# First delta product ahead of x's transposes, and the experts' start positions summed on VectorE

## The reference

```
out  = einsum(x, W_base) + b_base                       # btc,oc->bto
h    = einsum(x, As)                                    # btc,erc->bter
x    = x + out + einsum(h, Bs, w) * 2.0                 # bter,eor,be->bto

w, sel = top_k(softmax(cond), 2);  w = w / w.sum()      # per sequence
dense_w = zeros(B, 8).at[rows, sel].add(w)
mlp(x, g, u, d) = (gelu_tanh(x @ g) * (x @ u)) @ d      # 128 -> 512 -> 128
x = x + mlp(x, shared) + sum_e dense_w[:, e] * mlp(x, expert e)
```

## Time and profile before

| what | us |
|---|---|
| device time, three runs | 130.02, 130.43, 130.75 (median 130.43) |
| device time of the profiled execution | 130.85 |
| its span | 129.2 |
| TensorE busy | 124.9 (97% of the span), 873 products |
| VectorE busy | 90.2 (70%) |
| ScalarE busy | 72.0 (56%) |
| GpSimd busy | 61.8 (48%) |

### The profile page before, as it was taken

The page is one execution under the profiler, slowest core; times in us unless marked ns, Lnnn a source line. Parts: engine busy times, 40 slices in busy tenths (PEclk is TensorE's granted clock), DMA queues, the critical chain, the costliest instruction groups (busy, mean ns, idle before and its releaser), DMA issues.

```text
span 129.2 us, 3167 instructions
## 1 busy us (share of the span) xinstructions
PE 124.9 (97%) x873; PEld 113.9 (88%) x873; DVE 90.2 (70%) x177; ACT 72.0 (56%) x136; POOL 61.8 (48%) x111
## 2 busy tenths in 40 slices
PE   6999999999999999999999999999999999999991
PEld 5948887878887888998999999999999999999990
DVE  1686798769979999633377768667867686766731
ACT  2349677976956877113466485648565846711110
POOL 5364974463797877453344632643364604610000
PEclk9999999999999999999999999999999999999999
DMA  2998778799100077679745686558699960014922
GB/s 39 266 329 313 218 272 219 296 310 292 36 3 0 5 173 239 233 275 411 302 183 223 244 322 231 208 223 325 228 315 306 402 211 0 3 26 141 263 82 61
DMA packets 14524, 26.56 MB, mean 206 GB/s; under 512 B 2224, under 2 KB 7600, under 8 KB 12976
## 3 DMA queue, kind: packets, MB, share of 16 engines
q1 hardware_dynamic: 14048, 26.28, 60.8%
q10 hardware_dynamic: 464, 0.13, 0.4%
HBM read 12.52 MB, written 1.31 MB: 107 GB/s over the span
## 4 chain that ended last, share of the span: by engine, by line
PE 97%; issue 0%; DVE 0%; DVEq 0%
PE bank L1059 11%; PE bank L1100 9%; PE bank L1101 9%; PE bank L1099 9%; PE bank L1081 6%; PE bank L1004 6%; PE bank L1005 6%; PE bank L1006 6%; PE bank L1121 5%; PE bank L1122 4%; PE bank L1123 4%; PE bank L1022 3%; PE bank L928 3%; PE bank L936 3%; PE bank L1023 3%; PE bank L1024 3%
## 5 line engine op out<-in xcount | busy, mean ns | idle before, releaser
L558 ACT ACTIVATE work<-bank 128x512 f32<-128x512 f32 x48 | 28.7, 599 | 38.3 <-PE bank L1101 17.6
L720 DVE TENSOR_TENSOR bank<-bank,work 128x512 f32<-128x512 f32 x40 | 27.9, 698 | 18.3 <-PE bank L1101 13.1
L739 DVE TENSOR_TENSOR hT_lo<-bank,hT_hi 128x512 fp32r<-128x512 f32 x40 | 27.3, 682 | 1.0 <-issue 0.5
L1099 PE MATMUL bank<-xp,wst 128*128 128x256 f32 x96 | 27.2, 284 | 0.0
L1101 PE MATMUL bank<-xp,wst 128*128 128x256 f32 x96 | 27.2, 283 | 0.0
L1100 PE MATMUL bank<-xp,wst 128*128 128x256 f32 x96 | 27.2, 283 | 0.0
L485 POOL TENSOR_TENSOR wstd<-wexd,wstd 128x512 fp32r<-128x512 f32 x12 | 15.6, 1296 | 24.0 <-ACT wstd L600 24.0
L567 ACT CAST hT_hi<-bank 128x512 fp32r<-128x512 f32 x40 | 23.3, 583 | 1.8 <-DVE bank L720 1.8
L1099 PEld LDWEIGHTS bank<-xp,wst 128*128 128x128 f32 x96 | 18.4, 192 | 0.0
L1100 PEld LDWEIGHTS bank<-xp,wst 128*128 128x128 f32 x96 | 18.4, 192 | 0.0
L1101 PEld LDWEIGHTS bank<-xp,wst 128*128 128x128 f32 x96 | 18.4, 192 | 0.0
(11 more groups left out here) (156 smaller groups left out, 214.0 us busy)
## 6 DMA issues: line engine op xcount, KB each, us to landing
wst<-wex SPq DMA_DIRECT2D x12, 1024.0 KB, 5.0
raw_ex<-n_L_cond_skill_gate_dram SPq DMA_DIRECT2D x8, 256.0 KB, 3.5
raw_ex<-in_L_cond_skill_up_dram SPq DMA_DIRECT2D x8, 256.0 KB, 4.1
sst<-n_L_cond_skill_gate_dram SPq DMA_DIRECT2D x8, 256.0 KB, 3.5
sst<-in_L_cond_skill_up_dram SPq DMA_DIRECT2D x8, 256.0 KB, 4.0
xn<-in_x_dram SPq DMA_DIRECT2D x4, 256.0 KB, 4.8
out_dram<-xT SPq DMA_DIRECT2D x4, 256.0 KB, 2.7
sst<-_L_cond_shared_gate_dram SPq DMA_DIRECT2D x1, 256.0 KB, 4.9
```

Source lines behind the costliest of these rows:

```text
L558: act.activation(gelu_sb[q], gate_ps[q][:, :], ACT.Gelu_apprx_tanh).then_inc(gelu_done, 1)
L720: dve.tensor_tensor(up_ps[u][:, :], up_ps[u][:, :], gelu_sb[q], ALU.mult).then_inc(h_done, 1)
L739: dve.tensor_tensor(hT_lo[:, q, :], up_ps[u][:, :], f32(hT_hi[:, q, :]), ALU.subtract).then_inc(lo_done, 1)
L1099: pe.matmul(of_c, w_hi, x_hi, start=True, stop=False)
```

## The change

It makes two edits. In the first stretch of TensorE's program `delta_w(0)` stands ahead of x's first transposes and `delta_w(1)` ahead of `sort_counts`, and the warm-ups are (3, 1, 2). With it VectorE makes `w_eff(1)` right after `w_eff(0)` and the router's small operations after both, and ScalarE copies the counts after `copy_xT(0)` and a table load. The second edit computes the start positions with two small VectorE steps over `below`, a table of constants, and the products in `sort_starts`, `half`, `par` and ScalarE's copy of the result are gone. The second count product has its operands exchanged, so each partition holds all experts' sizes. The scratch of the new steps lies in `rows`, which is written later.

The diff, without most of its changes of semaphore counts and of declarations:

```diff
@@ -33,7 +33,7 @@
     NC = I // P
-    WARM_UP = (4, 2, 1)
+    WARM_UP = (3, 1, 2)
     DN = NC * H
...
@@ -92,6 +90,10 @@
         rows = sb("rows", [B, 2, 3, 32])
+        spare = rows[:, :, :, :].rearrange("b k v n -> b (k v n)")
+        n_ge = spare[:, 0:64].rearrange("b (e r) -> b e r", e=8)
+        in_front = spare[:, 0:144].rearrange("b (i f e) -> b i f e", i=2, f=9)
         wlist = sb("wlist", [P, 32])
...
@@ -333,23 +334,21 @@
             pool.memset(ones[:, :], 1.0).then_inc(const_fill, 1)
-            pool.memset(upick[:, :, :], 2.0).then_inc(const_fill, 1)
+            pool.memset(below[:, 0, :, :], 2.0).then_inc(const_fill, 1)
+            pool.memset(below[:, 1, :, :], 1.0).then_inc(const_fill, 1)
             pool.memset(ltri[:, :], 1.0).then_inc(const_fill, 1)
             pool.wait_ge(const_fill, 1)
             pool.affine_select(out=ident[:, :], in_=ident[:, :], compare_op=ALU.not_equal, fill=1.0,
                                base=0, pattern=[[-1, P]], channel_multiplier=1).then_inc(consts, 1)
             pool.iota(iota[:, :], pattern=[[1, 32]], base=0, channel_multiplier=0,
                       allow_small_or_imprecise_dtypes=True).then_inc(consts, 1)
-            pool.wait_ge(const_fill, 4)
+            pool.wait_ge(const_fill, 5)
             pool.affine_select(out=ltri[:, :], in_=ltri[:, :], compare_op=ALU.is_gt, fill=0.0,
                                base=0, pattern=[[1, B]], channel_multiplier=-1).then_inc(consts, 1)
-            pool.affine_select(out=upick[:, 0, :], in_=upick[:, 0, :], compare_op=ALU.is_gt, fill=0.0,
-                               base=0, pattern=[[1, 8]], channel_multiplier=-1).then_inc(consts, 1)
-            pool.affine_select(out=upick[:, 1, :], in_=upick[:, 1, :], compare_op=ALU.is_gt, fill=0.0,
-                               base=0, pattern=[[-1, 8]], channel_multiplier=1).then_inc(consts, 1)
-            pool.affine_select(out=upick[:, 2, :], in_=upick[:, 2, :], compare_op=ALU.is_equal, fill=0.0,
-                               base=0, pattern=[[-1, 8]], channel_multiplier=1).then_inc(consts, 1)
+            for i in range(2):
+                pool.affine_select(out=below[:, i, :, :], in_=below[:, i, :, :], compare_op=ALU.is_gt, fill=0.0,
+                                   base=0, pattern=[[1, 9], [-1, 8]], channel_multiplier=0).then_inc(consts, 1)
             pool.iota(thr[:, :], pattern=[[2, 8]], base=2, channel_multiplier=0,
...
@@ -396,22 +395,18 @@
             pool.memset(base[:, :, :], 0.0).then_inc(base_zero, 1)
-            pool.wait_ge(sort_sum, 2)
-            pool.tensor_scalar(par[:, :], half[:, :], -2.0, None, ALU.mult).then_inc(sort_step, 1)
-            pool.wait_ge(sort_step, 4)
-            pool.tensor_tensor(par[:, :], par[:, :], rank_n[:, 1, :], ALU.add).then_inc(sort_step, 1)
-            pool.wait_ge(sort_sb, 2)
-            pool.tensor_tensor(pos_e[:, 0, :], rank_n[:, 0, 0:8], starts[:, 2, :], ALU.subtract).then_inc(sort_step, 1)
-            pool.tensor_tensor(pos_e[:, 1, :], rank_n[:, 0, 0:8], starts[:, 0, :], ALU.add).then_inc(sort_step, 1)
+            pool.wait_ge(sort_sum, 5)
+            pool.tensor_tensor(pos_e[:, 1, :], rank_n[:, 0, 0:8], starts[:, 0, 0:8], ALU.add).then_inc(sort_step, 1)
+            pool.tensor_scalar(pos_e[:, 2, :], starts[:, 1, 0:8], starts[:, 0, 8:9], None, ALU.add).then_inc(sort_step, 1)
+            pool.wait_ge(sort_step, 5)
+            pool.tensor_tensor(pos_e[:, 2, :], pos_e[:, 2, :], pos_e[:, 1, :], ALU.subtract).then_inc(sort_step, 1)
             pool.wait_ge(sort_step, 6)
-            pool.tensor_scalar(pos_e[:, 0, :], pos_e[:, 0, :], 0.0, None, ALU.is_equal).then_inc(sort_step, 1)
+            pool.wait_ge(sort_sum, 6)
+            pool.tensor_tensor(pos_e[:, 2, :], pos_e[:, 0, :], pos_e[:, 2, :], ALU.mult).then_inc(sort_step, 1)
+            pool.wait_ge(sort_step, 7)
+            pool.tensor_tensor(pos_e[:, 3, :], pos_e[:, 1, :], pos_e[:, 2, :], ALU.add).then_inc(sort_step, 1)
             pool.wait_ge(sort_step, 8)
-            pool.tensor_tensor(pos_e[:, 2, :], pos_e[:, 0, :], starts[:, 1, :], ALU.mult).then_inc(sort_step, 1)
-            pool.wait_ge(sort_step, 9)
-            pool.tensor_tensor(pos_e[:, 3, :], pos_e[:, 1, :], pos_e[:, 2, :], ALU.add).then_inc(sort_step, 1)
-            pool.wait_ge(sort_step, 10)
             pool.tensor_tensor(pos_ke[:, :, :], memb[:, :, 0:8],
...
@@ -531,11 +526,11 @@
                                bias=bias[:, 0:1]).then_inc(x1hi_ready, 1)
-            act.wait_ge(sort_mm, 1)
-            act.copy(rank_n[:, :, :], count_ps[0:B, 0:2 * B].rearrange("p (a b) -> p a b", a=2)).then_inc(sort_sb, 1)
             copy_xT(0)
             act.wait_ge(exp_done, 1)
             act.activation(rt[:, 24:25], rt[:, 8:9], ACT.Gelu_apprx_tanh).then_inc(gelu_table, 1)
+            act.wait_ge(sort_mm, 1)
+            act.copy(rank_n[:, :, :], count_ps[0:B, 0:2 * B].rearrange("p (a b) -> p a b", a=2)).then_inc(sort_sb, 1)
             copy_xT(1)
...
@@ -579,19 +574,15 @@
                     gelu(t, c % 2)
-                    if g == 0 and c == 2:
-                        act.wait_ge(sort_mm, 2)
-                        act.copy(starts[:, :, :], start_ps[0:B, 0:24].rearrange("p (a b) -> p a b", a=3)
-                                 ).then_inc(sort_sb, 1)
                     if c > 1 or (c == 0 and g > 0):
                         split_h_hi(t - 1, (t - 1) % 2, (t - 1) % 3)
                     if g == 0 and c >= 2:
                         split_hi(0, c - 2)
                     if g == 1 and c == 2:
-                        act.wait_ge(sort_mm, 3)
+                        act.wait_ge(sort_mm, 2)
                         act.copy(left_rank[:, :], rank_ps[0:B, 0:4]).then_inc(sort_sb, 1)
                     if g == 3 and c == 0:
-                        act.wait_ge(sort_mm, 4)
+                        act.wait_ge(sort_mm, 3)
                         act.copy(wlist[:, :], list_ps[:, 64:96]).then_inc(lists_ready, 1)
...
@@ -694,15 +685,15 @@
             scale_B(1)
-            router_weights()
             dve.wait_ge(setup_ps, 3)
             dve.wait_ge(consts, 1)
             dve.tensor_tensor(wT[:, :], bank[6][:, 0:H], ident[:, :], ALU.add).then_inc(setup_sb, 1)
             dve.wait_ge(setup_sb, 3)
             w_eff(0)
+            w_eff(1)
+            router_weights()
             router_sum()
-            w_eff(1)
             w_eff(2)
...
@@ -769,14 +760,26 @@
                     if g == 0 and c == 0:
-                        dve.wait_ge(consts, 8)
+                        dve.wait_ge(consts, 7)
                         dve.wait_ge(sort_sb, 1)
-                        dve.tensor_tensor(n_ge[:, :, :],
-                                          rank_n[:, 1, :].rearrange("p (b a) -> p b a", a=1).to_broadcast([B, B, 8]),
-                                          thr[:, :].rearrange("p (a r) -> p a r", a=1).to_broadcast([B, B, 8]),
+                        n = rank_n[:, 1, 0:8]
+                        dve.tensor_tensor(n_ge, n.rearrange("p (e a) -> p e a", a=1).to_broadcast([B, 8, 8]),
+                                          thr[:, :].rearrange("p (a r) -> p a r", a=1).to_broadcast([B, 8, 8]),
                                           ALU.is_ge).then_inc(sort_sum, 1)
                         dve.wait_ge(sort_sum, 1)
-                        dve.tensor_reduce(half[:, :], n_ge[:, :, :], AXIS_X, ALU.add).then_inc(sort_sum, 1)
+                        dve.tensor_reduce(twos_odd[:, 0, :], n_ge, AXIS_X, ALU.add).then_inc(sort_sum, 1)
+                        dve.wait_ge(sort_sum, 2)
+                        dve.scalar_tensor_tensor(twos_odd[:, 1, :], twos_odd[:, 0, :], -2.0, n, ALU.mult, ALU.add
+                                                 ).then_inc(sort_sum, 1)
+                    if g == 0 and c == 1:
+                        dve.wait_ge(sort_sum, 3)
+                        dve.tensor_tensor(in_front, twos_odd[:, :, :].rearrange("p i (a e) -> p i a e", a=1)
+                                          .to_broadcast([B, 2, 9, 8]), below[:, :, :, :], ALU.mult).then_inc(sort_sum, 1)
+                        dve.wait_ge(sort_sum, 4)
+                        dve.tensor_reduce(starts[:, :, :], in_front, AXIS_X, ALU.add).then_inc(sort_sum, 1)
+                        dve.scalar_tensor_tensor(pos_e[:, 0, :], twos_odd[:, 0, :], 2.0, rank_n[:, 0, 0:8],
+                                                 ALU.mult, ALU.is_equal).then_inc(sort_sum, 1)
                     if g == 0 and c == 2:
...
@@ -939,21 +942,14 @@
             def sort_counts():
-                pe.wait_ge(consts, 8)
+                pe.wait_ge(consts, 7)
                 pe.wait_ge(sort_step, S_MEMB)
                 pe.matmul(count_ps[0:B, 0:B], ltri[:, :], memb_sum[:, :], start=True, stop=True)
-                pe.matmul(count_ps[0:B, B:2 * B], memb_sum[:, :], ones[:, 0:B], start=True, stop=True).then_inc(sort_mm, 1)
-            def sort_starts():
-                pe.wait_ge(sort_sum, 2)
```

(20 more changed lines are left out.)

39 lines of the change are left out of this document (18 added, 21 removed).

## The result

| | median, us | range, us | runs |
|---|---|---|---|
| kernel before | 130.38 | 130.02 to 130.75 | 4 |
| changed kernel | 131.50 | 131.12 to 131.71 | 4 |

The ratio is 1.0082, interval 1.0065 to 1.0098. The forecast was 130.3, "the same", with 131.0 as the top of the range. The changed kernel's profiled execution took 131.12 (span 129.4), 0.27 more than the one of before. The two traces can explain this 0.27; the other 0.8 of the medians' 1.1 is in neither trace, and needed experiments.

What follows compares the result with a forecast made beforehand. TensorE's row of work was taken to bound the kernel, with 97% of the chain. Terms -0.39 + 0.15 + 0.15 = -0.09 on 130.85, on the median 130.34, gave 130.3; range 129.5 to 131.0.

Steps and rivals of the forecast that it cites:

- the same: Whole kernel: the forecast verdict, no change that measurement can tell (about 0.5%, 0.65 us); chance 0.62.
- What bounds the kernel: Whole kernel: TensorE holds 97% of the chain of waits; other engines' idle time matters only if it delays TensorE.
- Step 1: First ten microseconds: delta(0) waits for sB(0) with its weight load exposed, 0.3 us of slow time lost, costing +0.15.
- rival A: Start of the kernel: the clock rises sooner or unseen gaps close, giving 129.6; chance 0.24.
- rival B: TensorE before 5.5 us: emptier early work makes the clock rise later; a rise at 10 gives 131.4; chance 0.11.
- Step 2: Around 20 us: the small start-position products leave TensorE and the first down product gets cheaper, -0.39.
- Step 3: Around 20 us: VectorE's added small operations delay lo(1), so TensorE waits some 0.2 at the second down product; +0.15.
- Rival C: Around 20 us: VectorE is the limit, lo(1) and lo(2) both 0.4 late, giving 130.6 to 130.8; chance 0.07.
- So it happens once: After the second down product: the next lo has some 0.2 to spare, so VectorE's lateness does not recur.
- GpSimd's part priced at nothing: GpSimd's queue: two operations fewer ahead of pos_ke, which comes no later, and constants ready long before needed; no cost.

Runs made afterwards that it cites:

- e5: Changed kernel with one wait added, so GpSimd starts x's fourth group only after VectorE's first pack; median 130.37 us, ratio to before 0.9932.
- e12: Changed kernel timed again as it is, twelve executions; median 131.18 us.
- e10: Kernel before with only the sort edit (start positions on VectorE) and GpSimd's wait for the first pack; median 130.21 us, ratio 0.9943.
- e9: Kernel before with GpSimd's wait for the first pack and nothing else; median 130.24 us, ratio 0.9941.
- e11: Kernel before with only the edit of the first stretch and GpSimd's wait for the first pack; median 130.66 us, ratio 0.9976.
- e6: Kernel before with the sort edit, warm-ups 3, 1, 2 and GpSimd's wait for the first pack; median 129.39 us, ratio 0.9891.
- e8: Kernel before with warm-ups 3, 1, 2 and GpSimd's wait for the first pack; median 130.41 us, ratio 0.9961.
- e18: e5 again, unchanged, as a control; median 130.25 us, ratio to before 0.9968.
- e16: e6 again, unchanged; median 129.43 us, ratio to before 0.9940.
- e2: Kernel before with only the edit of the first stretch, sort products left on TensorE; median 131.28 us, ratio 1.0055.
- e7: Kernel before with two otherwise unused fills of 0.09 us ahead of VectorE's first pack; median 130.96 us, ratio 1.0010.
- e14: e6 with the router's small operations moved behind w_eff(1); median 131.02 us, ratio to before 1.0022.

## Why the prediction was wrong

- **What bounds the kernel:** right, and too easily carried on. "Past its first product TensorE hardly waits for anybody" held for one execution with a margin of 0.02 us at 43.5. The earlier trace rows show that nobody was late, not how nearly.
- **Step 1, the order of the first products, +0.15:** the local sum was right (+0.14 read, some 0.25 with the earlier start of that execution taken out; the wait for sB(0) and the exposed load were there). It failed as a picture: it took the rise at 8 us as fixed. It moves between executions with the same first instructions, from 4.9 (e5) to 8.9 (e12), and the executions of the changed kernel spread over 2 us. The times of rival A (an early rise can be used, 129.6) and rival B (a late one, 131.4) both occur in different executions of the changed kernel: e12's run from 129.54 to 131.87. B had 0.11. B named two places where TensorE stands empty, at 3 and at 5.2 us; which of them delays the rise, if either, stays open.
- **Step 2, the start positions, -0.39:** right. Without the collision in either, the sort edit shortens the middle stage by 0.19 (e10 against e9), 0.38 (e5 against e11) and 0.44 (e6 against e8); -0.39 and the 0.03 of step 3 make a gain of 0.36. The device times scatter too much to show it: e10 is 0.03 below e9, e6 is 1.0 below e8.
- **Step 3, what VectorE takes over, +0.15:** right place, start times within 0.1, right wait (0.18), too dear: 0.03 on TensorE, since the load had been early. Rival C didn't happen.
- **The step that failed the sum** is the last sentence of step 3 and the one on GpSimd behind it: "So it happens once", and GpSimd's part priced at nothing. Both asked only whether somebody comes later. GpSimd came half a microsecond *earlier* from 30.6 us on, and at 43.5 that put its operation in front of VectorE's pack: 0.5 in the changed kernel, with the whole sum being 0.09. (The reason given for GpSimd's nothing was wrong as well: `pos_ke` came 1.0 later, not "no later". That cost nothing, since lo(2) stood ahead of VectorE's reduction.)

With the collision out of both, the changed kernel lies at 130.37 and 130.25 (e5, e18) and the kernel before at 130.24 (e9), on three different chips: "the same" would have been right, as a median of a wide spread, and partly by luck, since the rise was taken as fixed. As measured, the collision gives 0.5; that the other 0.6 is a draw of four executions from the upper part of e12's spread is argued, not shown.

The fastest version is e6 and e16: the sort edit, warm-ups 3, 1, 2, the hold, and x's transposes first. 129.39 and 129.43, six executions each, 1.1% below the kernel before on one chip and 0.6% on another.

## What to carry to other kernels

An instruction that comes earlier is a change too: list what on VectorE and GpSimd will now overlap that did not, above all tiny operations with two SBUF inputs beside long ones, and look at who starts first and by how much. Where a start of 0.02 us decides half a microsecond, write the order down with a wait. And a trace shows one execution: before pricing work at the clock's lower level, ask how the sum looks with the rise 3 us earlier or later, and time often enough to see the spread.

## What the runs showed of the hardware

- An operation of 16 integers took 0.17 us, or 0.96, 1.19 and 1.26 when it began 0.37, 0.13 and 0.05 us behind an operation of GpSimd that lasts 1.3 (changed kernel, e2, e7): it ended when that one did. A router operation of 2 numbers per sequence took 0.15 or 1.22. The cast of 64 integers ahead of the pack, with one input, kept its 0.20 beside the same operation of GpSimd (43.27 in the changed kernel).
- In this kernel TensorE's clock went from its lower level (1.2 GHz; a transpose 421 ns) to its upper (2.4 GHz; 272 ns) between 4.8 and 8.9 us; with the same instructions up to the rise, near 4.9 in e5 and 8.9 in e12. An order of work without a hole at 5 us did not fix the moment: near 4.8 in e6 and 8.9 in e14, both with x's transposes right behind the warm-ups.
- The kernel before runs at 130.3 on some chips and 130.9 on others, and one wait in GpSimd's queue brings it to 130.24 on the second kind. That the race at 43.5 us is what differs between the chips is inferred from this; no trace of the kernel before comes from a chip of the second kind.
